# Global attention: the rotated half by copies instead of a second projection, and one merged buffer of sums

## What is computed

```python
def _rotate_half(x):
    x1, x2 = jnp.split(x, 2, axis=-1)
    return jnp.concatenate((-x2, x1), axis=-1)
...
q = (x @ Wq).reshape(b, n, HEADS, DIM_HEAD).transpose(0, 2, 1, 3)
kv = (x @ Wkv).reshape(b, n, 2 * KV_HEADS, DIM_HEAD)
...
q = q * cos + _rotate_half(q) * sin
k = k * cos + _rotate_half(k) * sin
...
dots = jnp.einsum('bhid,bhjd->bhij', q, k) * SCALE
attn = jax.nn.softmax(dots, axis=-1)
out = jnp.einsum('bhij,bhjd->bhid', attn, v)
out = out.transpose(0, 2, 1, 3).reshape(b, n, HEADS * DIM_HEAD)
return out @ Wo + bo
```

## Time and profile before

| | before |
|---|---|
| median of 3 runs | 3910.77 us |
| the profiled execution | 3910.19 us |
| its span, first to last instruction | 3908.4 us |
| granted TensorE clock over the span | 0.943 |
| TensorE matmuls busy | 3422.6 us (88%) |
| VectorE busy | 2563.9 us (66%) |
| ScalarE busy | 1828.0 us (47%) |
| GpSimd busy | 1582.6 us (40%) |
| GpSimd's adds of exponents, L2924 | 320, 776.2 us |
| VectorE's adds of exponents, L2924 | 128, 194.8 us |
| VectorE's row maxima, L2972 | 512, 624.5 us |
| ScalarE's exponents, L2877 | 512, 524.4 us |

### The profile page before, as it was taken

One profiled execution on the slowest core, in us unless ns is written; L12 is line 12 of the kernel. 1 busy time (PEld: TensorE's weight loads), 2 busy tenths in 40 slices (PEclk: granted clock), 3 DMA queues, 4 the chain that ended last, 5 costly groups with the idle time before them and its releaser, 6 DMA issues. The chain is left out here.

```text
span 3908.4 us, 61702 instructions
## 1 busy us (share of the span) xinstructions
PE 3422.6 (88%) x23454; PEld 2133.2 (55%) x23454; DVE 2563.9 (66%) x4849; ACT 1828.0 (47%) x3254; POOL 1582.6 (40%) x1085
## 2 busy tenths in 40 slices
PE   6999999999857326999669999999999999978997
PEld 4777777777746214777523333333333333336776
DVE  4565656565655666777657776767677766757775
ACT  2343434444323113999523333333333343339996
POOL 1212121212104002666325555656555566646664
PEclk9999999999978557999879999999999999989998
DMA  2000000000010001000100000000000000010000
GB/s 93 1 1 1 1 1 1 1 1 1 1 51 3 5 0 44 2 2 2 38 1 1 1 1 1 1 1 1 1 1 1 1 1 1 1 44 2 2 2 12
DMA packets 21485, 31.44 MB, mean 8 GB/s; under 512 B 8418, under 2 KB 17932, under 8 KB 19724
## 3 DMA queue, kind: packets, MB, share of 16 engines
q1 hardware_dynamic: 21196, 27.52, 2.3%
HBM read 26.46 MB, written 1.05 MB: 7 GB/s over the span
## 5 line engine op out<-in xcount | busy, mean ns | idle before, releaser
L2924 POOL TENSOR_TENSOR global_acc_pool<-global_acc_pool,global_probs 128x1024 f32<-128x1024 f32 x320 | 776.2, 2426 | 470.7 <-ACT global_probs L2877 453.9
L2877 ACT ACTIVATE global_probs<-global_ps 128x1024 f32<-128x1024 f32 x512 | 524.4, 1024 | 883.3 <-PE global_ps L2750 822.2
L2972 DVE TENSOR_REDUCE global_part<-global_ps 128x2 f32<-128x1024 f32 x512 | 624.5, 1220 | 429.7 <-PE global_ps L2732 429.6
L2750 PE MATMUL global_ps<-global_q,global_k 64*128 64x512 f32 x2048 | 522.4, 588 | 0.0
L2761 PE MATMUL global_ps<-global_probs,global_v 128*64 128x512 f32 x2048 | 495.7, 605 | 0.0
L2732 PE MATMUL global_ps<-global_khh,global_qhh 64*128 64x512 f32 x1024 | 324.9, 631 | 35.7 <-DVE global_part L2972 33.6
L994 DVE COPY_PREDICATED delta_Y<-delta_tri,delta_ps 128x512 f32<-128x512 uint32 x192 | 140.3, 731 | 290.9 <-PE delta_ps L533 290.9
L2748 PE MATMUL global_ps<-global_mrow,global_first 64*128 64x512 f32 x1024 | 323.6, 629 | 0.0
L900 POOL TENSOR_TENSOR delta_gm<-C_tile,delta_g 128x1024 f32<-128x1024 f32 x16 | 30.3, 1896 | 719.2 <-PE delta_ps L453 685.5
L2761 PEld LDWEIGHTS global_ps<-global_probs,global_v 128*64 128x64 f32 x2048 | 124.2, 136 | 282.6 <-issue 161.5
L2732 PEld LDWEIGHTS global_ps<-global_khh,global_qhh 64*128 64x128 f32 x1024 | 97.9, 188 | 322.7 <-DVE global_part L2972 259.1
(11 more groups left out here) (594 smaller groups left out, 6810.6 us busy)
## 6 DMA issues: line engine op xcount, KB each, us to landing
delta_cw<-in_conv_taps SPq DMA_DIRECT2D x4, 1024.0 KB, 10.5
local_tab<-in_rot_tables SPq DMA_DIRECT2D x2, 2048.0 KB, 12.3
local_tab<-in_rot_tables SPq DMA_DIRECT2D x2, 1536.0 KB, 7.9
localw_wqkv<-in_L_ffn_wqkv SPq DMA_DIRECT2D x2, 768.0 KB
delta_wqkvz<-in_L_attn_a_W_qkvz SPq DMA_DIRECT2D x1, 1024.0 KB, 5.5
local_tab<-in_rot_tables SPq DMA_DIRECT2D x2, 512.0 KB, 4.1
global_cos<-in_rope_cos SPq DMA_DIRECT2D x2, 512.0 KB, 10.5
global_sin<-in_rope_sin SPq DMA_DIRECT2D x2, 512.0 KB, 11.7
```

The costliest lines, as they stand in the source:

```text
L2750: mm = pe.matmul(ps[:, 2 * (at % 2) + s, :], k2[own, group_of(u) % 2, P * k:P * k + P], q[own, u % 3, :], start=False, stop=True)
L2877: act.activation(probs[:, at % RING, :], ps[:, 2 * (at % 2):2 * (at % 2) + 2, :].rearrange("p b n -> p (b n)"), ACT.Exp).then_inc(S["probs ...
L2924: ins = eng.tensor_tensor(sums[:, u % 2, :], sums[:, u % 2, :], probs[:, at % RING, :], ALU.add)
L2972: dve.tensor_reduce(part[:, u % 2, r % SLOTS, :], ps[:, 5:7, :], X_AXIS, ALU.max)\
```

## The change

The second projection is gone, with its weights. After the one projection of a block, ScalarE copies the four groups of 32 partitions of bank 7 into an SBUF tensor `swapped`, each into the place of its neighbour, two of them with scale -1 (`swap_halves`): for a query block in span 0, ahead of the exponents of the unit's slot 0 (and ahead of the rounding of a key block), for a key block in span 5. VectorE then makes both products in the same span, cos out of PSUM and sin from `swapped`, and joins them one span later. The projections of spans 1 and 6 fall away.

GpSimd adds VectorE's buffer of sums to its own (`merge_sums`) after it has added slot 1 of the next unit, and TensorE multiplies this one buffer by ones: two products in place of four. `out_sums` waits for the merge, and stands ahead of the second rough product of span 1, no longer behind it.

```diff
-            def project(pe, key, part_no):
-                n = 2 * rope_no[key] + part_no
+            def project(pe, key):
+                n = rope_no[key]
                 if n:
                     pe.wait_ge(S["proj_read"], n)
...
             def out_sums(pe, u):
-                pe.wait_ge(S["sum_step"], (u + 1) * len(dve_adds))
-                pe.wait_ge(S["odd_step"], (u + 1) * (TILES - len(dve_adds)))
+                pe.wait_ge(S["merged"], u + 1)
                 if u + 3 < UNITS:
-                    pe.wait_ge(S["proj_read"], 2 * rope_no["q", u + 3] + 2)
+                    pe.wait_ge(S["proj_read"], rope_no["q", u + 3] + 1)
...
-                for n, sums in enumerate((acc, acc_pool)):
-                    for s, own in enumerate((UP, DOWN)):
-                        mm = pe.matmul(ps[own, 7, :], ones[:, 0:HD], sums[:, u % 2, BLK * s:BLK * s + BLK],
-                                       start=(n == 0), stop=(n == 1))
+                for s, own in enumerate((UP, DOWN)):
+                    mm = pe.matmul(ps[own, 7, :], ones[:, 0:HD], acc_pool[:, u % 2, BLK * s:BLK * s + BLK],
+                                   start=True, stop=True)
...
-                        if j < 2 and u + 2 < UNITS:
+                        if j == 0 and u + 2 < UNITS:
                             pe.wait_ge(S["mrow_ready"], u + 1)
-                            project(pe, ("q", u + 2), j)
+                            project(pe, ("q", u + 2))
...
-                        if j in (5, 6) and next_keys(u):
+                        if j == 5 and next_keys(u):
...
+                        if j == 1 and u:
+                            out_sums(pe, u - 1)
                         if at + 1 + AHEAD < UNITS * SLOTS:
                             rough_scores(pe, at + 1 + AHEAD)
-                        if j == 1 and u:
-                            out_sums(pe, u - 1)
...
+                def swap_halves(key):
+                    n = rope_no[key]
+                    act.wait_ge(S["proj_ps"], n + 1)
+                    if n:
+                        act.wait_ge(S["rope_ready"], n)
+                    for a in range(4):
+                        b = a ^ 1
+                        ins = act.activation(swapped[32 * a:32 * a + 32, :], ps[32 * b:32 * b + 32, 7, :], ACT.Copy,
+                                             scale=1.0 if a % 2 else -1.0)
+                    ins.then_inc(S["swap_ready"], 1)
...
                 for b in range(QB):
+                    swap_halves(("k", 0, b))
...
-                round_rope(("q", 0))
-                round_rope(("q", 1))
+                for u in range(2):
+                    swap_halves(("q", u))
+                    round_rope(("q", u))
                 for u in range(UNITS):
                     for j in range(SPANS):
+                        if j == 0 and u + 2 < UNITS:
+                            swap_halves(("q", u + 2))
+                        if j == 5 and next_keys(u):
+                            swap_halves(next_keys(u))
...
+                def merge_sums(u):
+                    pool.wait_ge(S["sum_step"], (u + 1) * len(dve_adds))
+                    pool.wait_ge(S["odd_step"], (u + 1) * (TILES - len(dve_adds)))
+                    pool.tensor_tensor(acc_pool[:, u % 2, :], acc_pool[:, u % 2, :], acc[:, u % 2, :], ALU.add)\
+                        .then_inc(S["merged"], 1)
...
+                    if at % TILES == 1 and at >= TILES:
+                        merge_sums(at // TILES - 1)
                     if at % TILES == 5 and at >= TILES:
                         normalize_context(at // TILES - 1)
+                merge_sums(UNITS - 1)
                 normalize_context(UNITS - 1)
...
+                def rotate(key):
+                    n = rope_no[key]
+                    dve.wait_ge(S["swap_ready"], n + 1)
+                    if n:
+                        dve.wait_ge(S["rope_ready"], n)
+                    dve.tensor_tensor(rot[:, 0, :], ps[:, 7, :], cos[:, columns(key)], ALU.mult)\
                         .then_inc(S["proj_read"], 1)
+                    dve.tensor_tensor(rot[:, 1, :], swapped[:], sin[:, columns(key)], ALU.mult)\
+                        .then_inc(S["rot_ready"], 1)
...
-                dve.tensor_scalar(wkr[:, :, :, 0:32], wk[:, :, :, 32:64], -1.0, None, ALU.mult)
-                dve.tensor_copy(wkr[:, :, :, 32:64], wk[:, :, :, 0:32])
-                dve.tensor_scalar(wqr[:, :, 0:32], wq[:, :, 32:64], -SCALE, None, ALU.mult)
-                link(dve.tensor_scalar(wqr[:, :, 32:64], wq[:, :, 0:32], SCALE, None, ALU.mult))
```

More of the change, by code:

```diff
@@ L2664, in sb @@
             return ctx.enter_context(nc.sbuf_tensor(f"{tag}_{name}", shape, dt))
-        wq, wqr = sb("wq", [P, H, HD]), sb("wqr", [P, H, HD])
-        wk, wkr = sb("wk", [P, KV, 2, HD]), sb("wkr", [P, KV, 2, HD])
+        wq = sb("wq", [P, H, HD])
+        wk = sb("wk", [P, KV, 2, HD])
         wv = sb("wv", [P, KV * HD])
@@ L2677, in grouped_attention @@
         q, qhh = sb("q", [P, 3, BLK]), sb("qhh", [P, 2, BLK], F32R)
-        rot = sb("rot", [P, 2, BLK])
+        rot, swapped = sb("rot", [P, 2, BLK]), sb("swapped", [P, BLK])
         part, nmx = sb("part", [P, 2, SLOTS, 2]), sb("nmx", [P, P])
@@ L2715, in project @@
                     p, cols = u // QB, slice(BLK * (u % QB), BLK * (u % QB) + BLK)
-                    weights = (wq, wqr)[part_no][:, 2 * p:2 * p + 2, :].rearrange("d h e -> d (h e)")
+                    weights = wq[:, 2 * p:2 * p + 2, :].rearrange("d h e -> d (h e)")
                 else:
                     cols = slice(BLK * key[2], BLK * key[2] + BLK)
-                    weights = (wk, wkr)[part_no][:, key[1], :, :].rearrange("d a e -> d (a e)")
+                    weights = wk[:, key[1], :, :].rearrange("d a e -> d (a e)")
                 pe.matmul(ps[:, 7, :], weights, xnT[:, cols], start=True, stop=True).then_inc(S["proj_ps"], 1)
@@ L2948, in _, with columns @@
                 link = counted(dve, S["dve_step"])
-                def rotate(key, part_no):
-                    n = 2 * rope_no[key] + part_no
+                def columns(key):
                     block_no = key[1] % QB if key[0] == "q" else key[2]
-                    cols = slice(BLK * block_no, BLK * block_no + BLK)
-                    dve.wait_ge(S["proj_ps"], n + 1)
-                    if part_no == 0 and n:
-                        dve.wait_ge(S["rope_ready"], rope_no[key])
-                    dve.tensor_tensor(rot[:, part_no, :], ps[:, 7, :], (cos, sin)[part_no][:, cols], ALU.mult)\
+                    return slice(BLK * block_no, BLK * block_no + BLK)
+                def rotate(key):
[4 more added lines that the diff above has]
+                    dve.tensor_tensor(rot[:, 0, :], ps[:, 7, :], cos[:, columns(key)], ALU.mult)\
                         .then_inc(S["proj_read"], 1)
+                    dve.tensor_tensor(rot[:, 1, :], swapped[:], sin[:, columns(key)], ALU.mult)\
+                        .then_inc(S["rot_ready"], 1)
                 def join_rotated(key):
                     n = rope_no[key]
-                    dve.wait_ge(S["proj_read"], 2 * n + 2)
+                    dve.wait_ge(S["proj_read"], n + 1)
+                    dve.wait_ge(S["rot_ready"], n + 1)
                     if key[0] == "q":
@@ L3017, in _ @@
                 for key in rope_order[:QB + 2]:
-                    rotate(key, 0)
-                    rotate(key, 1)
+                    rotate(key)
                     join_rotated(key)
@@ L3033, in _ @@
                             part_max(at + AHEAD)
-                        if j < 2 and u + 2 < UNITS:
-                            rotate(("q", u + 2), j)
-                            if j == 1:
-                                join_rotated(("q", u + 2))
+                        if j == 0 and u + 2 < UNITS:
+                            rotate(("q", u + 2))
+                        if j == 1 and u + 2 < UNITS:
+                            join_rotated(("q", u + 2))
                         if j == 2 and u:
@@ L3041, in _ @@
                             add_rows(u - 1)
-                        if j in (5, 6) and next_keys(u):
-                            rotate(next_keys(u), j - 5)
-                            if j == 6:
-                                join_rotated(next_keys(u))
+                        if j == 5 and next_keys(u):
+                            rotate(next_keys(u))
+                        if j == 6 and next_keys(u):
+                            join_rotated(next_keys(u))
                         if j == 7 and u + 1 < UNITS:
```

16 lines of the change are left out of this document (7 added, 9 removed).

## The result

The changed kernel takes 3922.05 us (median of 8 runs, 3917.25 to 3928.33) where the kernel before takes 3910.83 (8 runs beside them): ratio 1.0031, 95% interval 1.0021 to 1.0042. It is slower, by 11 us or 0.3%; forecast was no change, at 3908. The profiled execution took 3920.09 us (span 3918.3).

What follows compares the result with a forecast made beforehand. TensorE bounds the units, busy 1222.3 of 1230 us. Terms +3.5 + 1.6 + 2.0 - 6.1 - 0.7 = +0.3; with unit 0 and the last two units -1.9 us, giving 3908, range 3880 to 3928.

Steps and rivals of the forecast that it cites:

- part 4: VectorE and GpSimd exclude each other in the units; the merge comes late and 1.79 of 2.15 us return as TensorE's wait.
- 17 units not after a key unit: Span 2 starts at 12.37 in place of 12.73, 0.36 us less a unit: 6.1 us gained.
- 12 units after one: ScalarE's key rounding delays the exponents; merge ends at 11.55, span 2 starts 0.17 us later: 2.0 us lost in all.
- second projection of 12 key units: Span 5 and after: held sin product makes TensorE wait 1.1 of the 1.15 us gained; 0.7 us gained in all.
- Part 1: The second projection goes: 30 query and 12 key projections inside the units at 1.15 take 48.3 us from TensorE.
- Part 2: One pair of sums goes, the other moves ahead: span 1 takes 5.77 in place of 6.77, 1.00 less in 31 units.
- Prologue: First projection starts 1.2 earlier, but blocks take 5.2 us each on ScalarE; VectorE's first maximum comes 3.5 us later.
- Part 3: ScalarE's four copies at 0.62 each, bounds 0.49 and 0.80; slot 0's exponents start at 2.60, alone costing nothing.
- rival (c): Slower: copies across partitions take longer, in 29 units and 6 prologue blocks; 3933 at 0.80 each; 25 in 100.
- Rival (a): VectorE's sin product and add of slot 15 run beside GpSimd, so exclusion costs less: 3859 us; 17 in 100.
- Rival (b): The merge never holds TensorE in the units: 74 us less, 3836; 3 in 100.
- The end: After the last unit the merge adds 2.44 and the missing pair takes 0.9 away: transpose 1.6 us later.

Runs made afterwards that it cites:

- filling the hole: Changed kernel, and the late merge, each with two more pairs of products of ones ahead of TensorE's wait for the merge: 3908.21 us (0.9990) and 3945.17 us (1.0080).
- merge ahead of slot 0: Changed kernel with VectorE's add of slot 15 at the start of span 0 and GpSimd merging before its copy of slot 0: 3841.63 us, ratio 0.9820.
- keys later: On top of merge ahead of slot 0, a key block's swap goes behind span 5's exponents, its products to span 6, its join to span 7: 3838.95 us.
- keys later and the prologue: Keys later, plus the swap waiting for the sin product alone and each prologue rounding put behind the next swap: 3832.81 us, ratio 0.9804.
- slot 15 early: Changed kernel with VectorE's add of slot 15 moved to the start of span 0, merge still behind GpSimd's add of slot 1: 3870.62 us, ratio 0.9896.
- the swap alone: Changed kernel with copies and new rotation kept but sums unmerged as before, four products behind the second rough product: 3901.56 us, ratio 0.9964.
- the merge alone: Kernel before, second projection kept, with only GpSimd's merge and the single pair of sums ahead of the second rough product: 3893.46 us, ratio 0.9950.
- the key rounding moved: Changed kernel with ScalarE rounding the key block in span 2 of the next unit, no longer in span 0: 3906.83 us, ratio 0.9980.
- the late merge: The merge alone, with GpSimd multiplying its buffer by ones ahead of each merge, 2.4 us, no change of values: 3966.27 us, ratio 1.0149.

## Why the prediction was wrong

**The step that failed** is in part 4, where TensorE "stands in the wait for the merge" and the wait is priced at its length. It was right as a length: forecast 9.29 to 11.08, measured 9.26 to 10.97. It was wrong as a price, because it took for granted that TensorE goes on at the clock it had. The units of the earlier trace rows ran at 1.00 with TensorE idle for 8 of 1230 us; they tell nothing of the clock with a hole of 1.7 in each. The table ahead of the prediction had the warning beside it: 0.943 over the whole span, so there were places where the clock was lower. The five falls cost 14.3 us in the profiled execution, where the sum has nothing for the clock. All signs that the prediction named came out (30 waits, 1.7 to 2.2 each; VectorE's adds of slot 15 at 2.25; units 0.5 shorter, and 0.2 longer after key units), and none of them looks at the clock. Shown by filling the hole: the two kernels with it give back 12 and 22 us of the stage with work added, and the changed one then has the ratio 0.9990, at 3908 us. That this is the very time of the forecast is partly luck: without its falls the stage would be 5.6 shorter than before where the sum has 1.9, and the filling and the rest of the program take that back.

The prediction left open whether GpSimd's one-input copy blocks the sin product. It does; in unit 3, after a key unit, the product takes 1.39 us in place of 0.7:

```profile
2163.72 1.04 POOL L2934 COPY global_acc_pool<-global_probs 128x1024 f32<-128x1024 f32 x1 [5.35 <-ACT global_probs L2884]
2163.91 1.39 DVE L2983 TENSOR_TENSOR global_rot<-global_swapped,global_sin 128x512 f32<-128x512 f32 x1
```

The Trainium skill (SBUF — State Buffer, Who interferes with whom) states that a VectorE instruction with two SBUF inputs contends with a GpSimd instruction that reads SBUF; this trace agrees.

The rest of the sum, against the profiled executions, falls left out:

| term | forecast | measured |
|---|---|---|
| prologue to the first unit | +3.5 | +4.4 |
| unit 0 | -1.15 | 0.0 |
| 17 units not after a key unit | -6.1 | -8.5 |
| 12 units after one | +2.0 | +1.8 |
| second projection of 12 key units | -0.7 | -3.9 |
| unit 30 | -0.5 | -0.35 |
| last unit and end | +1.1 | +0.8 |
| falls of the clock | none | +14.3 |

**Part 1**: the size was off. A projection was put at 1.15, as 5.96 less a plain span of 4.81. But of the two matmul rows it ran between (2438.88 and 2443.69 in rows 2), the first begins with its weight load and the second 0.23 after it, as the weight loads of the kernel before show:

```profile
2438.88 0.19 PEld L2748 LDWEIGHTS global_ps<-global_mrow,global_first 64*128 64x128 f32 x2 [0.81 <-issue]
...
2443.46 0.19 PEld L2748 LDWEIGHTS global_ps<-global_mrow,global_first 64*128 64x128 f32 x2
```

From weight load to weight load the span is 4.58 and the projection 1.38. This is 0.23 too little for each of the 42 projections, 9.7 us in all. It gave 0.25 of the difference in each key unit, where the span ahead of the missing projection is 1.37 shorter and the next, by the maximum behind the held sin product, 1.06 longer (forecast 1.1). In the units about half of it is eaten up: with the sums ahead of the last maximum product, span 2 takes 4.71 and no longer 4.58, in every kernel that has them there. In unit 0 nothing came of the whole 1.38: it takes 41.25 after 41.21. Part of that is the clock of the prologue, which the sum has nowhere. The kernels with the swap have the same order of work in unit 0 up to its span 4, and with full clock from 1.0 us on it took 40.05 (merge ahead of slot 0), from 2.9 on 41.26 (keys later), and from 3.7 and 3.9 on 43.18 (keys later and the prologue) and 43.23 (slot 15 early). The kernel with the swap alone, 41.25 with full clock from 1.2 on, shows that this is not all of it.

**Prologue**: of the 0.9 above the forecast, 0.5 is a later load and not the change. In both kernels the weight instructions wait for the landing of the sin table, which came 20.5 us into the stage before and 21.0 after. Behind it the first projection starts 1.2 earlier, as forecast (0.8 in place of 2.0). The rest is in blocks of up to 5.34 where 5.2 was taken, and in two projections at half clock that take 2.05 and 2.07.

**Part 2** was right where nothing else is late: with the merge alone span 1 takes 5.81 (forecast 5.77).

**Part 3**: right. The four copies take 2.39, starts 0.60 apart (forecast 0.62), and so rival (c), which was slower by longer copies, named the right sign with a cause that isn't there. The change of partitions shows no cost of its own: a copy takes 0.59, and starts 0.01 after the last one has ended, like the second copy in rows 5.

**Part 4**: each time of the chain within 0.1 us. The sin product ends 5.19 after the unit's start (5.28), GpSimd's add 7.41 (7.50), VectorE's add of slot 15 8.50 (8.58), the merge 10.92 (11.02); after key units the merge 11.57 (11.55). By engine the groups of the page's view show it, where rows 4 had only single cases (columns: us busy, mean ns):

```profile
L2937 DVE TENSOR_TENSOR global_acc<-global_acc,global_probs 128x1024 f32<-128x1024 f32 x128 | 225.0, 1758 | 10.1 <-ACT global_probs L2884 10.1
L2983 DVE TENSOR_TENSOR global_rot<-global_swapped,global_sin 128x512 f32<-128x512 f32 x48 | 58.8, 1225 | 0.0
L2994 DVE TENSOR_TENSOR global_q<-global_rot 128x512 f32<-128x512 f32 x32 | 59.0, 1845 | 0.2
```

All three have bare durations of 1.22, 0.69 and 0.69. Rival (a), cheaper exclusion, is out by these lines. Rival (b), a merge that never holds TensorE, needs slot 15 early and the merge first: that version takes 3841.63. That this is near the 3836 given for it says little, since its order is another one.

**The end**: the merge takes 2.34 there and the transpose comes at 3476.89. That is 41.7 after the start of the last unit, where it was 40.9 before: 0.8 more, against 1.1 for end and last unit in the sum.

```profile
3473.37 2.34 POOL L2950 TENSOR_TENSOR global_acc_pool<-global_acc_pool,global_acc 128x1024 f32<-128x1024 f32 x1 [1.16 <-DVE global_acc L2937]
...
3475.76 1.08 PE L2776 MATMUL global_ps<-global_acc_pool,C_tile 128*64 128x512 f32 x4 [2.39 <-POOL global_acc_pool L2950]
...
3476.89 0.72 DVE L3018 STREAM_TRANSPOSE global_dent<-global_ps 128x512 f32<-128x512 f32 x1 [3.60 <-PE global_ps L2776]
```

**What stays open**: why the clock falls in one unit and not in the next with the same wait (3 of 29 waits of 1.71 with the key rounding moved, none of the 17 of that length in the changed kernel). The length does not decide it, but over the profiled executions the longer waits inside the units were hit more often: none of 29 waits of 0.5 to 1.05 (slot 15 early), 8 of 75 of 1.7 to 1.8, 7 of 14 of 2.2 to 3.0 (5 of 12 in the changed kernel, 2 of 2 with the late merge). So the number of falls could be forecast only as a chance, and these counts are of one execution for each kernel.

## What to carry to other kernels

Where an engine's work is cut on the path that sets the end, write down when its next input is ready. If the input comes later than the engine, part of the gain becomes a wait, and on a TensorE that was busy until then, put a price on the clock too: here some 1.5 to 3.8 us a fall behind waits of 1.7 to 3.0, in 3 to 7 of 29 to 31 such waits. The cure is the order of the producers (an add that is ready early must not stand behind a later one); where it can't be changed, useless products in the wait can be better than the wait (here by 12 and 22 us of the stage). And measure distances between like records, such as two weight loads.

## What the runs showed that was not expected

- Waits of TensorE of 1.7 to 3.0 us, about 30 in a stage, made its granted clock fall to half in 3 to 7 of them (3.4 us long in unit 4). Waits of 0.5 and 1.0 us in 29 units did not, in the one execution profiled.
- In three of the five falls of the changed kernel over half of the price is paid after it, at full clock: the late exponents bring GpSimd's add over a 0.43 us copy of VectorE, which then takes 2.57, and the next maximum is late (2.1 of 3.7 us in unit 4).
- Two changes of which each makes the kernel faster (0.9964 and 0.9950) make it slower together (1.0031). The one made a resource late, the other made its user early.
